# A recommender tower: the dense layers tile by tile inside the steps

## The reference

```python
e = stack([tbl_f[ids[:, f]] for f in range(24)], axis=1)      # [1024, 24, 16]
Xk, outs = e, []
for W in (W0, W1, W2):                                         # 24 x 24, 24 x 64, 24 x 64 pairs -> 64 units
    Wr = W.reshape(24, Xk.shape[1], 64)
    Xk = einsum('bfd,bhd,fho->bod', e, Xk, Wr)
    outs.append(Xk.sum(axis=2))                                # [1024, 64] of each layer
h = concatenate(outs + [dense_ctx], axis=1)                    # [1024, 208]
h = maximum(h @ W_top1 + b_top1, 0)                            # -> 512
h = maximum(h @ W_top2 + b_top2, 0)                            # -> 256
y = h @ W_top3                                                 # -> 1
```

## Time and profile before

| | |
|---|---|
| time, three runs | 456.87, 458.50, 462.52 us; median 458.5 |
| the profiled execution | 455.96 us, its span 454.1 us |
| PE busy | 373.9 us, 82% |
| DVE busy | 303.0 us, 67% |
| POOL busy (gathers of the embeddings) | 196.5 us, 43% |
| ACT busy | 127.6 us, 28% |
| mean granted TensorE clock | 0.962 of full |
| DMA | 64.76 MB, mean 143 GB/s |

### The profile page before, as it was taken

The page is one execution under the profiler, slowest core; times in us unless marked ns, Lnnn a source line. Parts: engine busy times, 40 slices in busy tenths (PEclk is TensorE's granted clock), DMA queues, the critical chain, the costliest instruction groups (busy, mean ns, idle before and its releaser), DMA issues. The chain is left out here.

```text
span 454.1 us, 6457 instructions
## 1 busy us (share of the span) xinstructions
PE 373.9 (82%) x2436; PEld 140.1 (31%) x2436; DVE 303.0 (67%) x305; ACT 127.6 (28%) x228; POOL 196.5 (43%) x196
## 2 busy tenths in 40 slices
PE   0005957995699899889998998899899998999997
PEld 0002201221134134312441243234333421443554
DVE  1003439887657995899599949994999498991000
ACT  1003000331222333234233333233414241127433
POOL 5777777787777877877707760000000000000000
PEclk9999975996889999999999999999989999999999
DMA  7000088366776787678766776876587558700000
GB/s 205 7 7 7 8 203 199 89 180 173 177 169 184 194 199 172 175 196 201 182 183 184 190 184 193 204 186 190 157 204 190 160 154 208 187 2 0 1 0 0
DMA packets 27203, 64.76 MB, mean 143 GB/s; under 512 B 7247, under 2 KB 10759, under 8 KB 27180
## 3 DMA queue, kind: packets, MB, share of 16 engines
q1 hardware_dynamic: 21036, 62.87, 51.4%
q0 software_dynamic: 6144, 1.59, 3.8%
HBM read 58.06 MB, written 6.38 MB: 142 GB/s over the span
## 5 line engine op out<-in xcount | busy, mean ns | idle before, releaser
L395 DVE TENSOR_TENSOR pairs<-spread,units 128x1024 f32<-128x1024 f32 x192 | 223.3, 1220 | 20.3 <-DMA units<-x_dram 13.1
L367 POOL DMA_INDIRECT emb<-in_tbl,ids_sb x192 | 196.3, 1023 | 74.2 <-issue 57.6
L593 PE MATMUL acc<-pairs,w_sb 128*64 128x512 f32 x768 | 200.3, 624 | 15.7 <-DVE pairs L395 14.6
L395 DVE TENSOR_TENSOR pairs<-turned,common 120x1024 f32<-120x1024 f32 x42 | 51.2, 1220 | 40.9 <-DMA turned<-x_dram 34.4
L593 PEld LDWEIGHTS acc<-pairs,w_sb 128*64 128x64 f32 x768 | 45.4, 139 | 106.9 <-DVE pairs L395 52.9
L593 PE MATMUL acc<-pairs,w 120*64 120x512 f32 x180 | 52.3, 666 | 9.9 <-DVE z L400 5.9
L567 PE MATMUL spread<-x0parts,sel 72*128 72x512 bf16 (+1 forms) x140 | 47.2, 426 | 11.2 <-DVE pairs L395 9.1
L455 ACT ACTIVATE x<-acc 128x512 f32<-128x512 f32 x31 | 18.6, 599 | 117.4 <-PE acc L593 117.4
L610 PE MATMUL misc<-ident_b,parts 128*72 128x128 bf16 x120 | 10.4, 235 | 39.9 <-DVE parts L297 37.0
L468 ACT ACTIVATE x0diag<-misc,mask 128x384 f32<-128x384 f32 x64 | 31.7, 611 | 15.2 <-PE misc L613 15.2
L628 PEld LDWEIGHTS misc<-x0diag,x2t 128*64 128x64 f32 x512 | 26.0, 137 | 18.8 <-issue 16.5
(11 more groups left out here) (38 smaller groups left out, 143.5 us busy)
## 6 DMA issues: line engine op xcount, KB each, us to landing
units<-x_dram SPq DMA_DIRECT2D x64, 512.0 KB, 7.5
turned<-x_dram SPq DMA_DIRECT2D x42, 480.0 KB
x_dram<-x SPq DMA_DIRECT2D x32, 128.0 KB
emb<-in_tbl,ids_sb POOLq DMA_INDIRECT x192
x_dram<-common SPq DMA_DIRECT2D x14, 96.0 KB
x_dram<-common SPq DMA_DIRECT2D x14, 56.0 KB
w_sb<-in_w SPq DMA_DIRECT2D x2, 384.0 KB
wt_sb<-in_wt SPq DMA_DIRECT2D x1, 512.0 KB, 5.5
```

The costliest lines, as they stand in the source:

```text
L367: pool.indirect_dma_start(out=e3[:, f, :], out_offset=None, in_=tables[f], in_offset=bass.IndirectOffsetOnAxis(ap=ids_sb[:, t, f:f + 1], a ...
L395: dve.tensor_tensor(pairs[buf][0:rows, :], source[0:rows, :], other[0:rows, h * HALF:(h + 1) * HALF], ALU.mult).then_inc(pairs_done, 1)
L593: last = pe.matmul(acc[half * H:(half + 1) * H, :], w, pairs[buf][0:rows, half * BLK:(half + 1) * BLK], start=first, stop=final)
```

## The change

The dense layers become three more kinds of side round, `("mlp", 1)`, `("mlp", 2)` and `("mlp", 3)`, one for each layer, for one tile of 128 columns. In steps 1 to 6 they stand at items 19, 21 and 27, for tile i - 1, and `x0t` moves from item 21 to item 23. In the last step layer 1 of tile 6 stands at item 23, and `x0t` moves from 21 to 19. The `zin_b` copies, two for the whole batch before, become two for each tile in the `take` of `z3`. Behind the last step stand the twelve rounds of TAIL: layers 2 and 3 of tile 6, the third layer of tile 7 and the three dense layers of tile 7. They go through the four `spread` banks in turn (`tail_bank`), each with the number of earlier rounds that must have been taken; the semaphores `z1_copied`, `mlp_ready` and `mlp_done` go.

```diff
-        13: ("gram", 2), 15: ("gram", 3), 17: ("z3", 0), 21: ("x0t", 0)}
+        13: ("gram", 2), 15: ("gram", 3), 17: ("z3", 0), 19: ("mlp", 1), 21: ("mlp", 2), 23: ("x0t", 0), 27: ("mlp", 3)}
...
-SIDE_LAST = {n: s for n, s in SIDE.items() if s[0] != "xt"}
+SIDE_LAST = {5: ("x2t", 0), 7: ("x2t", 1), 9: ("gram", 0), 11: ("gram", 1), 13: ("gram", 2), 15: ("gram", 3),
+             17: ("z3", 0), 19: ("x0t", 0), 23: ("mlp", 1)}
...
+TAIL = [("mlp", 2, TILES - 1, 0), ("x2t", 0, TILES, 0), ("x2t", 1, TILES, 0), ("mlp", 3, TILES - 1, 1),
+        ("gram", 0, TILES, 3), ("gram", 1, TILES, 3), ("gram", 2, TILES, 3), ("gram", 3, TILES, 3), ("z3", 0, TILES, 8),
+        ("mlp", 1, TILES, 9), ("mlp", 2, TILES, 10), ("mlp", 3, TILES, 11)]
...
+                    act.wait_ge(z1_done, 2 * i)
+                    for half in range(2):
+                        copy(zin_b[0:H, bass.ds(at, P)].rearrange("p (h e b) -> p e h b", e=2, b=BLK // D)[:, half],
+                             z1[half * H:(half + 1) * H, bass.ds((i - 1) * 2, 2), :])
...
+                elif kind == "mlp" and r == 3:
+                    copy(y[:, bass.ds((i - 1) * P, P)], src[0:1, 0:P]).then_inc(misc_free, 1)
+                elif kind == "mlp":
+                    if r == 1:
+
+                        act.wait_ge(mlp_in, 16 * 7)
+                    hidden, bias = ((h1, bt1_sb), (h2, bt2_sb))[r - 1]
+                    for m in range(hidden.shape[1]):
+                        last = act.activation(hidden[:, m, :], src[:, m * P:(m + 1) * P], ACT.Relu, bias=bias[:, m:m + 1])
                     last.then_inc(misc_free, 1)
...
+                elif kind == "mlp":
+                    at = (i - 1) * P
+                    if r == 1:
+
+                        pe.wait_ge(mlp_in, 16 * 7)
+                        for m in range(N1 // P):
+                            pe.matmul(dst[:, m * P:(m + 1) * P], wt1b_sb[:, m * P:(m + 1) * P], zin_b[:, bass.ds(at, P)],
+                                      start=True, stop=False)
+                            last = pe.matmul(dst[:, m * P:(m + 1) * P], wt1a_sb[:, m * P:(m + 1) * P],
+                                             z23[:, bass.ds(at, P)], start=False, stop=True)
+                    elif r == 2:
+                        for m in range(N2 // P):
+                            for k in range(N1 // P):
+                                last = pe.matmul(dst[:, m * P:(m + 1) * P], wt2_sb[:, k, m * P:(m + 1) * P], h1[:, k, :],
+                                                 start=(k == 0), stop=(k == N1 // P - 1))
+                    else:
+                        for k in range(N2 // P):
+                            last = pe.matmul(dst[0:1, 0:P], wt3_sb[:, k:k + 1], h2[:, k, :],
+                                             start=(k == 0), stop=(k == N2 // P - 1))
...
+            for o, (kind, r, i, need) in enumerate(TAIL):
+
+                pe.wait_ge(misc_free, base + max(need, o - 3))
+                if kind == "x2t":
+
+                    pe.wait_ge(x2_done, 2 * (TILES - 1) + r + 1)
+                side_round((kind, r), 0, i, tail_bank(o))
```

More of the change, by code:

```diff
@@ L175, in build_tower, with tail_bank @@
         zin_b = sb("zin_b", [H + D, B])
-        h2 = sb("h2", [P, N2 // P, B])
+        h1 = sb("h1", [P, N1 // P, P])
+        h2 = sb("h2", [P, N2 // P, P])
         y = sb("y", [1, B])
[L179 to L188, removed]
+        def tail_bank(o):
+            return spread[o // 2 % 2][:, o % 2 * BLK:(o % 2 + 1) * BLK]
         x0_dram = [nc.dram_tensor(f"x0_dram{h}", (X0_ROWS, HALF), F32).ap() for h in range(2)]
@@ L352, in _ @@
                     spread_units(t, t % 2, h)
-            sp.wait_ge(mlp_done, len(MLP_OUTS))
+            sp.wait_ge(misc_free, rounds(TILES - 1) + len(SIDE_LAST) + len(TAIL))
             sp.dma_start(out.rearrange("b o -> o b"), y[:, :]).then_inc(stored, 16)
@@ L455, in copy, with take @@
                 return act.activation(dst, src, ACT.Copy)
-            def take(number, what, slot, i):
+            def take(number, what, slot, i, src=misc):
                 kind, r = what
@@ L465, in take @@
                 elif kind == "x0t":
-                    x0 = misc[:, 0:GROUPS * F].rearrange("p (k e c) -> p k e c", k=GROUPS, e=2)
+                    x0 = src[:, 0:GROUPS * F].rearrange("p (k e c) -> p k e c", k=GROUPS, e=2)
                     for b in range(8):
@@ L482, in take @@
                     copy(gram[:, :, r * GK * 8:(r + 1) * GK * 8],
[L483 removed]
+                         src[:, 0:GK * 8 * NC].rearrange("p (b c) -> p c b", c=NC)).then_inc(misc_free, 1)
             def take_common(number, buf, h):
@@ L535, in _ @@
             steps(act, body)
[L539 to L544, removed]
             take_x2(item(TILES - 1, len(L2_ITEMS) - 1), 1)
             base = rounds(TILES - 1) + len(SIDE_LAST)
[L547 to L560, removed]
+            for o, (kind, r, i, _) in enumerate(TAIL):
+                take(base + o, (kind, r), 0, i, tail_bank(o))
         @block.tensor
@@ L601, in side_waits, with side_round @@
                     pe.wait_ge(x2_done, 2 * i)
-            def side_round(what, slot, i):
+            def side_round(what, slot, i, dst=misc):
                 kind, r = what
@@ L612, in side_round @@
                     for k in range(GROUPS):
-                        last = pe.matmul(misc[:, k * F:(k + 1) * F], group_cols(x0parts[slot][:, :], k),
+                        last = pe.matmul(dst[:, k * F:(k + 1) * F], group_cols(x0parts[slot][:, :], k),
                                          sel[:, SEL_FIELDS:SEL_FIELDS + F], start=True, stop=True)
@@ L617, in side_round @@
                     for k in range(4):
-                        last = pe.transpose(misc[:, k * P:(k + 1) * P], group_cols(x2[:, r, :], k), ident[:, :])
+                        last = pe.transpose(dst[:, k * P:(k + 1) * P], group_cols(x2[:, r, :], k), ident[:, :])
                 elif kind == "z3":
@@ L621, in side_round @@
                         for b in range(2):
-                            last = pe.matmul(misc[b * H:(b + 1) * H, 0:P // 2], w2_sb[:, c, :],
+                            last = pe.matmul(dst[b * H:(b + 1) * H, 0:P // 2], w2_sb[:, c, :],
                                              gram[:, c, b * (P // 2):(b + 1) * (P // 2)],
                                              start=(c == 0), stop=(c == L2_CHUNKS - 1))
+                elif kind == "mlp":
[16 more added lines that the diff above has]
+                                             start=(k == 0), stop=(k == N2 // P - 1))
                 else:
@@ L627, in side_round @@
                         for e in range(2):
-                            last = pe.matmul(misc[e * H:(e + 1) * H, k * 8 * NC:(k + 1) * 8 * NC],
+                            last = pe.matmul(dst[e * H:(e + 1) * H, k * 8 * NC:(k + 1) * 8 * NC],
                                              x2t[:, r * GK + k, :], x0diag[:, r * GK + k, e, :, :],
```

41 lines of the change are left out of this document (3 added, 38 removed).

## The result

The changed kernel took 441.75 us (median of four, 436.82 to 443.10) against 460.18 (456.87 to 462.52): a ratio of 0.9585, 95% interval 0.9499 to 0.9672. The first is 18.4 us less, the second 13.3. On those occasions single runs came out some 15 us under the rest of their kernel (564 for the kernel before, 575 for the changed one), and the medians given here lie among the others.

What follows compares the result with a forecast made beforehand. The prediction took a chain of transfers on SP's queue to set a step, with PE work in a row at the end. Its terms, 0.7 + 1.0 + 1.8 - 18.6 = -15.1 us, gave 443 us, range 437 to 453.

Steps and rivals of the forecast that it cites:

- What bounds the kernel: Steps: a chain of transfers on SP's queue sets the length; writes of x1 have 2.0 to 3.8 us of slack.
- The third case: Rival, steps: the write's 6.7 us are its own time, x1 of half 0 2.4 us late each step; 456, chance 0.10.
- What a tile costs PE: Dense layers of one tile on PE: 1.79, 1.98 and 0.5 us, together 4.2 us; narrow width nearly free.
- The rival with weights that are not hidden: Rival, narrow matmuls in the steps: weight loads show, 3.6 us a step, 21.6 in all; 465, chance 0.03.
- Steps 1 to 5: These steps: PE's added 4.2 us meets 4.4 us of slack; 0.15 us each, 0.7 us in all.
- The second case: Rival, steps: PE cannot hold the period and sets the step, 6 to 9 us in all; 450, chance 0.22.
- Step 6 and the last: Last two steps: 1.0 us for PE's lateness out of step 6, 1.8 us for layer 1 of tile 6.
- The end: From last contraction to last copy of y: 20.0 us instead of 38.6, with 1.4 for a lower clock.
- The sum: Whole kernel: 0.7 + 1.0 + 1.8 - 18.6 = -15.1 us, giving 443.
- the first case: The forecast itself, whole kernel: lateness of x1 hidden by the queue's slack, a gain of 11 to 18.6 us; chance 0.57.
- The slower case: Rival, steps: both halves of x1 late and exposed, 3.9 us a step, 23.4 in six; 465, chance 0.08.

Runs made afterwards that it cites:

- after_3: The changed kernel itself, unedited, run once more as the mark for another run: 587.03 us, beside the kernel before at 579.27.
- no_rounds: The changed kernel without any dense round for tiles 0 to 6, their y filled with constants: 557.32 us, 0.9627 of the kernel before.
- q_before: The kernel before with the two small writes of x1 issued from ACT's queue instead of SP's: 579.81 us against 579.35.

## Why the prediction was right, point by point

The forecast was -15.1 us and 443; measured were -18.4 with 441.75, and -13.3 with 443.06. Of the -18.4, 1.7 is that the kernel before came out at 460.18 and not at the 458.5 that I started from. The profiled executions show the terms.

**What bounds the kernel.** That PE and DVE had room in a step and a chain of transfers did not: right. Taking the rounds out (8.3 us for 29 us of PE's work) shows it. The explanation of the slack, a write that lies behind the read on the same queue, was wrong in its cause: the run with the writes on ACT's queue had the same 6.9 us. The third case had that part right, that the time is the write's own while the read is under way, and its consequence wrong: a write that comes later is also quicker. The slack is there all the same, and the runs with a late `x1` show where it ends, at 2.95 us from write to read. The chain is not of transfers alone: in the first link SP waits last for DVE (13.7 us in seven waits, above).

**What a tile costs PE.** Layer 1 took 2.0 us in step 6 (forecast 1.79) and layer 2 1.98 (the chain of the changed kernel has 16 records of it in 1.98 us in each step), nearly as forecast. The rival with weights that are not hidden falls. So the price of narrow matmuls that the Trainium skill gives in "TensorE: Matmul & The Clock Gate", section "Back-to-back issue gap", was not paid here, in steps between contractions with other weights either: 0.124 us a record at 128 columns against 0.429 at 512.

**Steps 1 to 5**, forecast 0.7 us. Measured over the five periods, from the read for tile 2 to that for tile 7: 219.8 us before, 221.1 and 223.7 after, 224.0 without any rounds. The cost lies inside the differences between executions, at most a few us; that the term itself was right cannot be shown. The window's PE share says how near it was: 43.5 of 43.7. The second case, PE over the period, needed only 0.6 to 1.2 us more work per step, as the doubled layer shows. I had written that PE's lateness would not be felt at `common`; SP does wait for it now, up to 1.8 us, and the period is no longer for it, since the write behind that wait then lands sooner (7.3 and 7.7 us to the read of `turned` in the last two periods, 8.1 and 8.7 before).

**Step 6 and the last**, forecast 1.0 + 1.8 = 2.8. From the last read of `turned` to the last contraction 60.3 us before, 64.0 after (63.9 the second time), 59.8 without the rounds: 3.6 to 4.2. This term was too small by 1 us: PE goes into the last step 1.8 us late (its first `x2t` round stands 34.7 us behind that read, 33.0 before), near the upper end of the 0 to 2 that I had allowed; as I had written, step 6 has no split and so no pause of 2.07 us to give. The last step then takes 2.0 us more, near the 1.8.

**The end**, forecast 20.0 us, measured 17.2 both times. This is the term that was most off. Of the 2.8 us, 1.4 were the clock: I took it to fall because PE works in turns with ACT, and it stayed at the upper level, 2.4 GHz, through 2.7 busy us in 4 and 1.8 in 3. It was not a fear without ground: with one bank it did fall in this end, but in the `gram` rounds and not in the turns with ACT. No run shows what layer 2's records cost at the lower level. The other 1.4: the `gram` rounds begin 3.6 us after the last contraction and not 4.2, and take 3.1 us and not 3.4; the four activations behind layer 1 take 1.14 us and not 1.57, and the last two 0.63 and not 0.8.

**The sum** on the traces: +1.3 (periods) + 3.7 - 21.3 = -16.3 us; the two spans differ by 19.1, and the remaining 2.8 us lie ahead of the first period, where no dense round has run yet. Executions of one kernel differ there by as much: the second profile of the changed kernel reaches the same read at 134.73 us and not at 131.10. That the sum of the terms comes so near is partly luck: the steps and the last step cost 1.5 us more than forecast and the end 2.7 less. The upper bound of the range, 453, does not follow from its own case either, which gives 458.5 - 18.6 + 1.8 + 9 = 450.7.

**The cases.** The write of `x1` was absorbed, as the first case had it. The slower case, both halves late and both paid for, did not occur. What no case of mine contained is the other kind of occasion, on which the change does not gain.

## What to carry to other kernels

Work that stands in a serial end can move into a loop at hardly a price as long as the engine that does it has slack in each turn. A share of busy time did not tell how much: PE had 40.5 of 43.7 us, took 4.2 us more, and the step stayed. How late one handover may come is read from the distance between what is handed over and who takes it: here from the write of `x1` to the read of `units`, 6.7 us against the 2.95 that the write needs. But it speaks for that handover only. The run with the rounds one item later has the long distance back with the same work on PE. What PE had left, about a microsecond in a step, only the run with more work on PE told.

An end that alternates between two engines gains from more banks: in a single bank this one was 6.5 us longer, some 5.2 by handovers and 1.3 by a clock that fell among them.

## What the hardware did that I had not expected

**A write is slow while another queue reads.** 128 KB twice took 2.95 us from issue to the dependent read on a quiet queue. While 1.4 MB of `turned` were being read it was 5.3 to 6.7 us from SP's queue (kernel before) and 5.7 to 7.5 from ACT's (four writes in the two runs).

**Two kinds of occasion.** The kernel before took 456 to 460 us on two and 579 on two. The three occasions of the experiments were on three chips: 579 us on two of them, 456 on the third. Whether it is the chip or the hour cannot be told. In the long ones DVE and ACT stand still for stretches, and PE for much of them, while POOL issues a tile's gathers. The changed kernel (after_3), in windows with the columns of the earlier trace rows, and its summed waits:

```profile
250.00:260.00 10.00, 5.53 (x18) 1.78 (x18) 0.81 (x1) 0.27 (x1) 7.56 (x9) 0.66 0.07 7
260.00:270.00 10.00, 2.36 (x12) 1.13 (x12) 3.29 (x3) 1.62 (x2) 2.55 (x3) 0.59 0.16 30
```

```profile
DVE pairs L385 <- remote: 141.6, 17, 36.0
ACT x L445 <- remote: 90.8, 5, 36.2
```

For ten microseconds DVE does 0.8 us of work, ACT 0.3, and the DMA engines move 7 GB/s, while POOL is busy; the profile names as the releaser only something that it cannot place ("remote"), with waits of up to 36 us. Once the gathers are through, steps take 45 us again. While they last, a step takes 59 us without the rounds (from split to split 58.5 to 59.9 in the trace of no_rounds, 58.3 to 60.1 in that of q_before) and 66.5 to 68.3 with them in three of the four such steps (after_3). So the change does not gain there: 587.03 against 579.27, 1.3% with no interval on record, and 575.06 against 563.87 by the shortest run of each. Without the rounds the time is 557.32, 0.9627 (0.9600 to 0.9653).

What holds the engines was not found. The rounds add instructions on PE and ACT to each step, and a delay in fetching code while the gathers run would fit, but no run here tests it. The trace of after_3 says only this much: from 246 to 266 us the packets are those of the gathers, but for five at its beginning, and the two queues that the profile calls "instruction" move none; ACT goes on at 265.8 and DVE at 266.7, some 2 us after the gathers' last packets.
